# A nine-slot ring in place of eight, and a shorter tail, in a four-layer graph network on one core

## The reference

```python
x = _layernorm(x + L0(x, adj, adj, W, a))    # softmax(scores from pos@hw, where adj>0) * adj @ (x@W)
x = _layernorm(x + L1(x, adj, W, b))         # relu(D^-.5 (adj+I) D^-.5 @ (x@W.T + b))
x = _layernorm(x + L2(x, adj, W, a))         # 4-head attention; (1-adj)*(-1e9) masks all but the row's largest entry
x = _layernorm(x + L3(x, adj, ...))          # sum_j adj[i,j] * gelu(s_i + d_j + b), then update, gelu, layer norm
```

## Time and profile before

| | |
|---|---|
| runs | 740.55 us median of three (735.58 to 743.03) |
| profiled execution | 736.55 us, of which the span from the first to the last instruction is 734.8 us |
| PE busy | 455.6 us (62%) |
| DVE busy | 503.4 us (69%) |
| ACT busy | 302.4 us (41%) |
| POOL busy | 378.1 us (51%) |
| mean granted TensorE clock | 0.761 of full speed |
| moved by DMA | 120.06 MB |

### The profile page before, as it was taken

One profiled execution on the slowest core, in us unless ns is written; L12 is line 12 of the kernel. 1 busy time (PEld: TensorE's weight loads), 2 busy tenths in 40 slices (PEclk: granted clock), 3 DMA queues, 4 the chain that ended last, 5 costly groups with the idle time before them and its releaser, 6 DMA issues.

```text
span 734.8 us, 6845 instructions
## 1 busy us (share of the span) xinstructions
PE 455.6 (62%) x1987; PEld 268.9 (37%) x1987; DVE 503.4 (69%) x1592; ACT 302.4 (41%) x362; POOL 378.1 (51%) x499
## 2 busy tenths in 40 slices
PE   4122015999959999999998368665345542675211
PEld 3121012444425565544446356443133321433100
DVE  3409904998971754997054586899898879877744
ACT  3566256356942523399836031123223223322213
POOL 7303630667561030667000665777777777777740
PEclk9555555799989999999999759877567766655555
DMA  8999993799980020499601232212221222212200
GB/s 330 336 427 424 401 413 77 270 406 401 392 336 10 1 76 1 151 383 424 275 1 43 66 91 63 51 48 59 56 55 50 56 58 58 56 48 58 55 15 14
DMA packets 33211, 120.06 MB, mean 163 GB/s; under 512 B 8704, under 2 KB 19892, under 8 KB 24148
## 3 DMA queue, kind: packets, MB, share of 16 engines
q1 hardware_dynamic: 20258, 80.99, 28.0%
q0 software_dynamic: 10176, 38.57, 16.7%
q10 hardware_dynamic: 2734, 0.01, 0.2%
HBM read 114.00 MB, written 5.55 MB: 163 GB/s over the span
## 4 chain that ended last, share of the span: by engine, by line
PE 39%; POOL 20%; DMA 15%; DVE 10%; issue 8%; ACT 3%; SPq 3%; ACTq 0%; POOLq 0%
PE ps L121 37%; POOL G L919 16%; DMA ring<-in_adjT_dram 13%; POOL Go L919 4%; SPq L839 2%; DVE agg L1824 1%; DMA xT_s<-in_xT_dram 1%; PE ps L1254 1%; PE ps L1260 1%; ACT binT L998 1%; DVE G L1821 1%; PE ps L1375 1%; DVE I L1500 1%; DVE listed L1708 1%; DVE V L1510 0%
## 5 line engine op out<-in xcount | busy, mean ns | idle before, releaser
L919 POOL DMA_INDIRECT G<-near,IX x154 | 159.5, 1036 | 46.9 <-issue 46.3
L121 PE MATMUL ps<-ring,hwu 128*128 128x512 f32 (+3 forms) x264 | 114.7, 588 | 1.0 <-ACT hwu L1011 1.0
L121 PE MATMUL ps<-ring,xT_s 128*128 128x512 f32 (+2 forms) x264 | 106.9, 547 | 1.8 <-DMA ring<-in_adjT_dram 1.8
L121 PE MATMUL ps<-ident,agg 128*128 128x128 f32 (+1 forms) x44 | 14.9, 435 | 123.4 <-DVE agg L1824 123.4
L1500 DVE FIND_INDEX8 I<-V,rows 128x8 uint32<-128x340 f32 (+2 forms) x176 | 88.2, 504 | 0.0
L1510 DVE MAX8 V<-rows 128x8 f32<-128x340 f32 (+2 forms) x176 | 85.6, 497 | 0.8
L121 PE MATMUL ps<-E,M 128*128 128x321 f32 (+2 forms) x192 | 66.1, 505 | 16.8 <-DVE IO L1716 9.9
L121 PEld LDWEIGHTS ps<-ring,hwu 128*128 128x128 f32 (+1 forms) x264 | 51.3, 204 | 64.4 <-issue 63.3
L998 ACT ACTIVATE binT<-ring 128x2708 bf16<-128x2708 f32 (+1 forms) x22 | 53.9, 2457 | 47.5 <-DMA ring<-in_adjT_dram 47.5
L942 POOL DMA_DIRECT2D rows<-in_adj_dram x18 | 10.8, 603 | 120.5 <-DVE I L1500 120.5
L121 PE MATMUL ps<-u,binT 128*128 128x4 bf16 (+1 forms) x484 | 18.2, 167 | 82.7 <-ACT binT L998 82.7
(11 more groups left out here) (255 smaller groups left out, 858.5 us busy)
## 6 DMA issues: line engine op xcount, KB each, us to landing
ring<-in_adjT_dram SPq DMA_DIRECT2D x48, 1354.0 KB, 16.8
rows<-in_adj_dram POOLq DMA_DIRECT2D x17, 1354.0 KB, 10.3
rows<-in_adj_dram SPq DMA_DIRECT2D x4, 1354.0 KB, 23.3
G<-near,IX POOLq DMA_INDIRECT x154, 2.5
xT_s<-in_xT_dram SPq DMA_DIRECT2D x1, 1354.0 KB, 6.0
near<-hwu SPq DMA_DIRECT2D x1, 1344.0 KB
out_dram<-yo SPq DMA_DIRECT2D x21, 64.0 KB, 1.7
near2f<-hwu SPq DMA_DIRECT2D x5, 256.0 KB
```

What stands on the lines that cost most here:

```text
L121: return pe.matmul(dst, lhsT, rhs, start=start, stop=stop, skip_group_check=True)
L919: pool.indirect_dma_start(out=dst, out_offset=None, in_=table, in_offset=bass.IndirectOffsetOnAxis(ap=index, axis=0), engine_sem=o_g).then ...
```

## The change

The ring gets a ninth slot; layer 1's tail takes five blocks in place of six. So each of layers 0 and 1 loads 13 blocks again in place of 14; `shares1_until` takes block 7 too; layer 1's plain loop takes blocks 8 to 16 in place of 7 to 15. The buffers of layers 2 and 3 are laid out anew so that `E2`, which is written while layer 1's tail still reads slots 8 and 0 to 3, lies over slots 4 to 7; `G3` now lies behind it and `Go` to `A` lie where `G3` began. `more` and `M` share their start.

```diff
-RING = 8
+RING = 9
...
-TAIL1 = 6
+TAIL1 = 5
...
         layer2_life.close()
-        G3 = sb("G3", [P, QUEUE3, TOP + 1, D], life=life)
         Go = sb("Go", [P, 2, CAP, D], life=life)
...
         A = sb("A", [P, CAP, 2 * P], life=life)
+        sb("to_ring_4", [P, 4 * N - 2 * NB * D - 40 * D], life=life)
...
         E2 = sb("E2", [P, NB, EW], life=life)
-        more = sb("more", [P, 2, NB, SEGS * 8], life=life)
+        G3 = sb("G3", [P, QUEUE3, TOP + 1, D], life=life)
+
+        sb("to_rows", [P, (RING + 1) * N - 4 * N - NB * EW - QUEUE3 * (TOP + 1) * D], life=life)
+        ranks_life = ExitStack()
+        more = sb("more", [P, 2, NB, SEGS * 8], life=ranks_life)
+        ranks_life.close()
         M = sb("M", [P, MSLOTS, CAP * P], life=life)
```

## The result

The changed kernel takes 728.33 us in the median of 16 runs (723.47 to 733.09), the kernel before 737.02 (732.28 to 746.55, 16 runs). The ratio is 0.9877, 95% interval 0.9851 to 0.9903: some 9 us less. The changed kernel was measured once more among the experiments (`again`): 0.9859 (0.9822 to 0.9896). The forecast was 10.3 us less, 730, with a range of 723 to 738.

A forecast was written before the change was run, and what follows sets the result against it. PE was taken to set the time in layers 0 and 1, with ring waits at three places. 9.3 + 1.1 + 0.35 - 0.4 = 10.3 us off the 740.55 median gave 730, range 723 to 738.

The forecast's parts named there:

- What bounds the kernel: Whole kernel: bytes bound the first pass, PE sets the time later, then gathers; the ring counts at three PE waits.
- half-gain rival: Layer 0's last reload: DMA is saturated, only a block's bytes are saved, 4 us idle stays; 5 us gain, 735.5; 15%.
- End of layer 0: PE's 7.35 us wait for block 0 goes, the clock stays at 1.00, the tail starts at 212.3; 9.3 us gained.
- VectorE did not become the bound: Rival, layer 0's tail: DVE or ACT become the bound, the gain falls to 6 or 7 us, 734; 10%.
- More: Rival: the clock dip in 250 to 257 goes with the halt and both bounds fall well; 13 us, 727.5; 7%.
- Block 7 and the cover of the first reload: Layer 0's tail: block 7 moves there at no cost; layer 1's first reload issues at 308.2, cover same or slightly longer.
- Layer 1's waits: PE's waits before block 8 (1.43 us) and block 20 (0.35 us) in layer 1 shrink; 1.1 and 0.35 us gained.
- Tail of five: Layer 1's tail: 5.1 us of PE work just covers a chunk's 5.1 us chain; 0.4 us lost.
- Layer 1's stream: Layer 1's reloads: twelve blocks at 429 GB/s take 39 us, ending near 350, before PE wants block 20.
- without DMA waits in the last blocks: Sign of being right, layer 1: ACT's last sign near 357.5, with no waits for loads in the last blocks.
- Places: New buffer places in SBUF and fewer DMAs: no wait added, no gain or loss, 1 us in the range.
- Slower: Rival, layer 1's five-block tail: PE waits in each slot and its clock falls; net +14 us, 754; 5%.

The follow-up runs named there:

- hold: The changed kernel with only layer 0's last reload (block 0) issued one block of TensorE later; 0.9928 of the kernel before.
- bytes11: The changed kernel with an extra unread load of 1.387 MB ahead of layer 0's last but one reload (block 1); 0.9966 of the kernel before.
- bytes0: The changed kernel with an extra unread load of 1.387 MB ahead of layer 0's first reload; 0.9891 of the kernel before.
- reload8: The changed kernel, but layer 1 loads block 8 again though it is still in the ring; 0.9957 of the kernel before.
- tail5: The kernel before, eight slots, with only layer 1's tail cut from six blocks to five; 1.0005 of the kernel before.
- tail4: The changed kernel with layer 1's tail cut once more, to four blocks; 0.9858 of the kernel before.
- before_again: The kernel before, unchanged, run as a kernel of its own on a slower chip; 1.0034 of the kernel before.

## Why the prediction was right

*What bounds the kernel.* Right. Layer 0's first large matmul starts 0.5 us apart, layers 2 and 3 took 328.8 us in both, and nearly all the difference lies where TensorE waited on the ring. Some slices were misread: PE stands at 5 and not 9 in slice 12, which is the halt itself, and at 8 in slice 22, and the 336 to 392 GB/s of the half-gain rival are slices 11 and 12 and not 10 and 11. None of it moves a number.

*End of layer 0.* Forecast 9.3 us; tail from 212.3, measured 212.26; main block at 206.5 and DVE's wait of 3, measured 206.55 and 2.77. From the first large matmul of layer 0 to the small matmuls of its tail, the four profiles of eight slots took 104.2 us on average and the seven of nine slots 95.7: 8.5 us. So the term was about 0.8 too high; the profile it was read from had the longest halt of the four (7.35 us for a mean of 6.75). The argument, that the first thirteen loads keep issue and landing, held. Its words made it a matter of issue time; hold, bytes11 and bytes0 show two causes of like size. Taking out one load does both, which is why the sum came out right.

*The rivals.* Half the gain fell: a halt of 4 us would have stayed, and the longest of seven is 0.9. Its mechanism is the other half of the sum. VectorE did not become the bound: it still waited 2.77 us for the sums. "More" tied the dip at 250 to the halt; bytes0, without a halt, has one at 246, so the 13 us of the profiled pair don't bear it out.

*Block 7 and the cover of the first reload.* That TensorE's sum is unchanged was right. "Cost nothing" rests on a block in the ring behind the early products, and reload8 shows the price without: 5.5 us. The reload went out at 306.41 (forecast 308.2), in again at 308.84.

*Layer 1's waits*, forecast 1.1 + 0.35 us. This is the term that was mis-sized most. Over the four profiles of eight slots the wait for block 8 is 0.6 on average, nine slots keep 0.1, and the clean stretch differs by 0.2 us in all. The prediction's shift of VectorE's rows by 7.4 us comes from no row; POOL's last row load of that stretch went out 9.1 us earlier (310.83 for 319.91) and the reload 6.5. The 1.43 was the largest of four and stood in the one profile that I had.

*Tail of five*, forecast 0.4 lost: no idle in its first slots, and tail5 as a whole 1.0005. The chain of 5.1 us is the bound, as tail4's 0.81 us shows.

*Layer 1's stream.* The twelve blocks were to land at 429 GB/s and end at 350. They took 45.6 us from issue (306.41) to the sign of block 20 (352.05), for which ACT waited 1.05 us; TensorE did not wait. So this term was too small by some 4 us, and "without DMA waits in the last blocks" was wrong. One window of 10 us had been taken for the whole stretch: in the changed kernel DMA moved 413 GB/s in 340 to 350 but 375 in 306 to 353. By the 358 GB/s that the Trainium skill states (page "SBUF — State Buffer", section "Summary: rules for kernel authors") the blocks, issued at 306.41, would end near 355, an estimate; the trace lies between the two. ACT's last sign still ended at 356.95 (forecast 357.5).

*Places*: nothing, as forecast. *Slower*: the clock stayed at 1.00 as long as the tail had matmuls on the ring's blocks, with five blocks and with four; the drops in its last slots cost about half a microsecond.

*The sum.* 8.5 of the first place and 0.2 behind it are 8.7, measured 9.1 (7.2 to 11.0). Eight slots lost 4.3 us to dips on average and nine 2.0; this is not in the 8.7, and whether it belongs to the change is not shown. That 730 came within 2 us of the measured 728.33 is in part luck: the starting median was 3.5 us too high (740.55 for 737.02) and the gain 1.2 to 1.6 too large, and the two offset each other. The profiled pair differs by 13.1 us: 0.5 before layer 0, 1.7 by the dip of the kernel before, 1.4 by its wait for block 8, and the rest, 9.5, of which 8.8 lie between layer 0's first large matmul and the small matmuls of its tail.

## What to carry to other kernels

A slot more in a ring is worth what the bound engine waits for the ring's last load, and both of its effects count: the load is issued a block earlier and stands behind a block less. Take both apart before putting the landing down to one. A halt's length in one profile is a draw: where several short waits are summed, ask for more than one profile, or expect the sum to be too high. When work is moved forward over a load, see that a block of work is left to cover its landing.

## What the runs showed of the hardware

TensorE's clock fell to 0.50 for short stretches also where TensorE had no idle, each costing 1.7 us or twice that, none to three a profile between 220 and 310 us. All of them began at the end of a run of small matmuls or just behind it. That is up to 5 us of a spread of 10 between runs of one kernel; why most such runs of matmuls pass without one stays open.

A load of 1.387 MB took 6.6 us to land in hold (issued at 205.62, its own queue worked off), at most 8.8 in after (199.98 to 208.8) and 11.3 in the kernel before (205.65 to 216.97, the load ahead of it landing near 208.98), in each case beside POOL's row loads.

Two chips were slower, in the last stage alone. On them the kernel before took 797.92 us (median of 23) and 800.02 (median of 17), and the stage behind the first list 378 to 392 us in four profiles, where it takes 320 to 326 elsewhere; the first 400 us were as on the others. The waits of that stage in before_again have these:

```profile
DVE A L1722 <- remote: 58.1, 4, 20.8
POOL Go L919 <- DVE msgo L1807: 53.5, 5, 14.1
```

VectorE waited 58.1 us in four waits of up to 20.8, put down to something that the trace doesn't show, and POOL's gathers waited for VectorE; neither is in the profile before. What made this stage slow there was not found. An earlier stage's own time, read from the trace, still told the kernels apart, where the ratio did not.
